# Two-layer Perceiver kernel: in the second attention GpSimd makes every low half, and the FFN weight rounding moves to the expert stage

## The reference, cut to what matters

```
x = x + _L0_xattn_ref(_layernorm(x), ctx_1024, mask, ...)      # attention 1, 6272 keys, masked
x = x + _L0_attn_ref(_layernorm(x), ...)                       # self-attention of the 64 tokens
x = x + _L0_ffn_ref(_layernorm(x), ...)                        # 8 experts, top 2 of a router
x = x + _L1_xattn_ref(_layernorm(x), ctx_1024, ...)            # attention 2: 6272 keys, no mask; then one over x
x = x + _L1_attn_ref(_layernorm(x), ...)                       # delta rule, FIR filters, gate
x = x + _L1_ffn_ref(_layernorm(x), W_in, b_in, W_out, b_out)   # weights rounded to 8 bits, activations to 16

def quantize_w8_per(w, axis):
    amax = jnp.clip(jnp.max(jnp.abs(w), axis=axis, keepdims=True), 1e-08, None)
    scale = 127.0 / amax
    w_q = jnp.clip(jnp.round(w * scale), -128.0, 127.0) / scale
```

## Time and profile before

| | |
|---|---|
| time, median of 3 runs | 408.29 us (408.04 to 408.51) |
| the profiled execution: its time, its span | 407.28 us, 405.5 us |
| busy: PE, DVE, ACT, POOL | 383.2, 286.6, 287.9, 237.8 us |
| attention 2, 222 to 342 us: busy PE, DVE, ACT, POOL | 116.84, 92.46, 106.12, 95.55 us |
| experts, 189 to 208 us: busy PE, DVE, ACT, POOL | 17.80, 11.09, 8.55, 1.65 us |

### The profile page before, as it was taken

One profiled execution on the slowest core, in us unless ns is written; L12 is line 12 of the kernel. 1 busy time (PEld: TensorE's weight loads), 2 busy tenths in 40 slices (PEclk: granted clock), 3 DMA queues, 4 the chain that ended last, 5 costly groups with the idle time before them and its releaser, 6 DMA issues.

```text
span 405.5 us, 11389 instructions
## 1 busy us (share of the span) xinstructions
PE 383.2 (95%) x4529; PEld 280.3 (69%) x4529; DVE 286.6 (71%) x724; ACT 287.9 (71%) x568; POOL 237.8 (59%) x198
## 2 busy tenths in 40 slices
PE   6988999999998999989999999999999999999996
PEld 3435777777776778954955767777777778867843
DVE  3788888888876777556767767877887776455544
ACT  3377888888787887736439989899889987534240
POOL 2497989999974659301006987887787659030000
PEclk9899999999999999999999999999999999999999
DMA  8899998989999997990004999999999999700000
GB/s 310 324 254 167 200 178 138 167 155 212 235 176 214 201 208 132 341 411 21 3 2 92 197 191 195 191 193 190 185 194 214 184 207 182 286 2 2 4 1 5
DMA packets 188390, 68.56 MB, mean 169 GB/s; under 512 B 183200, under 2 KB 183984, under 8 KB 187440
## 3 DMA queue, kind: packets, MB, share of 16 engines
q1 hardware_dynamic: 188048, 66.77, 81.5%
q10 hardware_dynamic: 288, 1.05, 0.7%
HBM read 21.90 MB, written 0.03 MB: 54 GB/s over the span
## 4 chain that ended last, share of the span: by engine, by line
PE 54%; DVE 16%; DMA 10%; POOL 6%; issue 6%; ACT 6%; SPq 2%; POOLq 0%; DVEq 0%; ACTq 0%
PE ps L522 19%; PE ps L490 15%; DMA probsT<-halves 8%; DVE probs L641 7%; POOL halves L594 4%; PE ps L502 3%; ACT probs L559 2%; PE ps L1104 2%; PE ps L766 2%; DMA moe<-in_ctxT 2%; ACT halves L566 1%; SPq L421 1%; PE ps L1212 1%; DVE halves L594 1%; PE ps L826 1%
## 5 line engine op out<-in xcount | busy, mean ns | idle before, releaser
L594 POOL TENSOR_TENSOR halves<-probs,halves 128x896 f16<-128x896 f32 x75 | 141.6, 1892 | 55.1 <-ACT halves L566 53.7
L522 PE MATMUL ps<-ctxN,probsT 128*128 128x128 f16 x2352 | 148.6, 219 | 4.5 <-DMA probsT<-halves 4.1
L522 PEld LDWEIGHTS ps<-ctxN,probsT 128*128 128x128 f16 x2352 | 139.4, 98 | 18.3 <-issue 7.8
L490 PE MATMUL ps<-ctxT_parts,GT_parts 128*128 128x512 f16 (+1 forms) x660 | 143.0, 353 | 5.4 <-DVE negmax L641 5.2
L559 ACT ACTIVATE probs<-probs,shifted 128x896 f32<-128x896 f32 x112 | 115.5, 1031 | 6.7 <-DVE shifted L646 6.7
L490 PEld LDWEIGHTS ps<-ctxT_parts,GT_parts 128*128 128x128 f16 x660 | 59.6, 98 | 57.0 <-DVE negmax L641 8.1
L566 ACT CAST halves<-probs 128x896 f16<-128x896 f32 x93 | 85.8, 923 | 0.0
L654 DVE SCALAR_TENSOR_TENSOR U<-U,alpha,ps 128x128 f32<-128x128 f32 x112 | 38.6, 345 | 54.5 <-PE ps L522 54.2
L641 DVE CUSTOM_DVE_ANT_0 probs<-ps,zero,negmax 128x896 f32<-128x896 f32 x56 | 67.5, 1205 | 1.6 <-POOL halves L594 1.2
L641 DVE CUSTOM_DVE_ANT_0 probs<-ps,maskb,negmax 128x896 f32<-128x896 f32 x56 | 67.5, 1205 | 1.6 <-issue 0.7
L556 ACT ACTIVATE alpha<-negmax 128x1 f32<-128x1 f32 x96 | 28.2, 294 | 37.0 <-DVE negmax L641 35.9
(11 more groups left out here) (369 smaller groups left out, 380.0 us busy)
## 6 DMA issues: line engine op xcount, KB each, us to landing
moe<-in_ctxT SPq DMA_DIRECT2D x7, 448.0 KB, 7.2
moe<-in_mask SPq DMA_DIRECT2D x6, 448.0 KB, 10.1
moe<-in_gateT SPq DMA_DIRECT2D x2, 1024.0 KB, 9.2
moe<-in_upT SPq DMA_DIRECT2D x2, 1024.0 KB, 10.9
moe<-in_downT SPq DMA_DIRECT2D x2, 1024.0 KB, 12.8
moe<-in_fir_long SPq DMA_DIRECT2D x1, 2048.0 KB, 10.3
probsT<-halves SPq DMA_TRANSPOSE x93, 4.7
wv<-in_wv SPq DMA_DIRECT2D x2, 512.0 KB, 6.8
```

Of the source, the lines that this page charges most:

```text
L490: ins = pe.matmul(ps[:, 2 * b + h, 0:width], GT_parts[:, g_part, r * P:(r + 1) * P], ctxT_parts[:, keys:keys + width], start=(g_part == 0 ...
L522: ins = pe.matmul(ps[:, bank, 0:D], probsT_parts[:, b, p_part, k * P:(k + 1) * P], ctxN_parts[:, at:at + D], start=(p_part == 0 and c_part ...
L594: eng.tensor_tensor(halves_of(L, n)[:, 1, :], probs[:, n % BUFS, :], halves_of(L, n)[:, 0, :], ALU.subtract).then_inc(lower_of(L, n)[0], 1)
```

## The change

Three edits. In attention 2, `on_vector` is False for every step, so the nine low halves that VectorE made (steps 15, 19, ... 47) are GpSimd's. The eight operations of `quantise_weights` leave the attention loop and stand in GpSimd's list behind norm 2's power and ahead of `bound_pool(pool, 1)`. And `wqi` and `wqo` are views of `maskb`, so the first operation waits for the last step of attention 1.

```diff
-RAMP = 12
@@
-        wqi = late(P, FT, D)
-        wqo = late(P, FT, D)
+        wqi, wqo = (maskb[:, 2 * k * FT * D:2 * (k + 1) * FT * D].bitcast(F32).rearrange("p (f d) -> p f d", f=FT)
+                    for k in range(2))
@@ def on_vector(L, n):
             if L == 0:
                 return n in (0, 2) or 4 <= n < 30 and n % 4 == 1
-            return n >= RAMP and n % 4 == 3
+            return False
@@ @block.gpsimd
                 if i == 3:
+                    pool.wait_ge(sem("negmax_ready"), STEPS)
+                    for stage in range(8):
+                        quantise_weights(stage // 4, stage % 4)
                     bound_pool(pool, 1)
                 norm_pool(pool, i)
@@
-                        if 12 <= n < 44 and n % 4 == 0:
-                            quantise_weights((n - 12) // 16, (n - 12) // 4 % 4)
```

## The result

The changed kernel takes 410.06 us (median of 7 runs, 408.83 to 412.06) against 408.29 of the kernel before (7 runs): ratio 1.0046, 95% interval 1.0029 to 1.0064, so slower by about 1.9 us. That is 0.26 us above the top of the predicted range. The profiled execution has 409.14 us, span 407.3; before it was 407.28 and 405.5. Its 1.8 us are what is to be explained.

The account below looks back on a forecast made before the run. TensorE was taken to bound the kernel, with attention 2's stalls due to DMA. The median 408.29 - 0.3 (attention 2) + 0.87 (L747 stopped) gave 408.85 us; the 8-in-10 range was 406.3 to 409.8.

Parts of the forecast that it names:

- What bounds the kernel, and attention 2's stalls: Whole kernel and attention 2: TensorE, busy 383.2 of 405.5 us, bounds it; the stalls are DMA's, low halves mostly without effect.
- an even supply: Attention 2, steps 15 to 43: low halves coming evenly from GpSimd could win 2.15 us at most.
- rival 2: Attention 2: stalls come from uneven low halves, so the change wins 2.15 us, 407.0 or 406.1 us in all; chance 0.20.
- -0.3 in attention 2: Steps 30 to 39: about half of 0.54 us won, where SyncE idled because a low half came late.
- L747 stopped, +0.87: Norm 2's xn on VectorE, held by GpSimd's first two-tensor weight operation, ends at 192.18 instead of 191.31: +0.87 us.
- Rival 1: Norm 2: L747 isn't stopped, as GpSimd starts later or no shared port is needed; 408.0 us, chance 0.20.
- The other VectorE operations ... Nothing for them: Router and its weights: VectorE's other two-input operations fall beside scalar GpSimd operations or have room, so they cost 0.
- Rival 3: Router: GpSimd's scalar operations also hold up VectorE's small ones; about +5.8 us, 413.8 us in all, chance 0.10.
- its sign: Router's end: TensorE's L1124 starting after 199 us in the later profile would show the router was stopped.

Follow-up runs that it names:

- e5: e4 with the nine low halves of attention 2 back on VectorE; 408.23 us, ratio 1.0016 to the kernel before.
- e4: Changed kernel, first four weight operations waiting for the router's choice, last four behind norm 3; 407.22 us, ratio 0.9991 to the kernel before.
- e8: e4 with nine one-column memsets in VectorE's list where its low halves had stood; 408.01 us, ratio 1.0006 to the kernel before.
- The probe: Kernel before, with single GpSimd operations (scalar, multiply, copy) beside chains of small VectorE operations added behind its result; no whole-kernel time given.
- e7: Changed kernel with each scalar weight operation replaced by two two-tensor multiplies, no rounding or clip; 412.94 us, ratio 1.0134 to the kernel before.
- e3: Changed kernel with the eight weight operations also waiting until VectorE's xn of norm 2 is done; 407.27 us, ratio 0.9989 to the kernel before.

## Why the prediction was wrong

**What bounds the kernel, and attention 2's stalls: right.** In the 103 us from step 0 to 43 an even supply won nothing: 103.04 before, 103.20 after, 102.79 to 103.84 in the other versions. The stalls stayed DMA's (2.5 us before and after), and rival 2 is out. The trace of the kernel before says more of them than the prediction did: its instruction queue q8 has a packet of some 16 KB every 10 to 12 us (at 246.9, 256.5, 268.25, 280.4, 292.1, 302.2, 313.6 and 323.3), and of the eight pv starts between steps 10 and 43 that come over 2.4 us behind the one before, seven (249.00, 258.59, 270.43, 282.54, 294.31, 315.64, 325.42) lie 2.0 to 2.2 us behind such a packet. The break of the earlier trace rows belongs to the third. That these fetches cause the stalls was not tested.

**-0.3 in attention 2: wrong in size and cause.** The stretch that I gave it to (steps 30 to 39) gained nothing. The last twelve steps gained 1.03 (medians: 1.0 between e5 and e4), by what the profiles show because VectorE's list became nine instructions shorter and a fetch of 8 KB fell between tiles. e8 takes it back with memsets. Without this gain, whose cause the prediction didn't have, the miss would have been some 1.3 us and not 0.26: that it is so small is luck.

**L747 stopped, +0.87: the mechanism right, the size 0.70.** `xn` took 1.05 us and ended 0.08 us behind GpSimd's multiply, where I had 0.21 from the larger low half. Rival 1 is out.

**"The other VectorE operations ... Nothing for them": this step failed.** It put the router's part at nothing, and the router cost 1.39 beyond its slack. It rested on "two-tensor operations of GpSimd stop such an operation of VectorE, scalar ones don't", and that on one row, the low half at 48.36, which lies wholly within 46.61 to 49.83. The probe shows that the middle is the one part of a scalar operation in which VectorE goes on. A row that I hadn't used says as much, the low half at a scalar operation's start. Timelines of the kernel before, VectorE and then GpSimd:

```profile
25.82 1.27 DVE L594 TENSOR_TENSOR halves<-probs,halves 128x896 f16<-128x896 f32 x1
```

```profile
25.22 3.22 POOL L1385 TENSOR_SCALAR maskb<-moe 128x896 bf16<-128x896 int32 x1
```

1.27 in place of 1.08, begun 0.6 us behind the start: stopped for 0.19, until some 0.8 us behind it. (In attention 2 itself the mean of 1.26 hid the same: VectorE's low halves at 258.87 and 297.26, each begun beside a low half of GpSimd, took 1.75 and 1.77, those that met none took 1.08.) Beside that I placed the router wrongly: it met the two multiplies as well, since once `xn` is late the router moves onto them. Measured 1.39 beyond the slack, 0.05 at the start of L1123, and 0.35 behind it. Predicted 0.57 in all; measured -1.03 + 0.16 + 2.49 + 0.25 of drift = 1.87.

**Rival 3** had the right place and threshold ("as soon as the router is over 1.3 us late": 1.29 is what was covered), and its sign came, TensorE's sum after 199 us (199.13). Its price was too large: with passages in the middle of scalar operations the router is 3.4 us late (2.7 by its own stops, 0.7 by `xn`), not 7. e7, in which every operation has two tensors, comes to its 5.8 (22.46 - 16.45 = 6.0), in part by the clock.

The rule of the Trainium skill ("SBUF — State Buffer", section "Who interferes with whom"), that the first holds the shared ports for its whole instruction, agrees with the multiply and the copy (1.20 and 0.53 us, to their ends). For the scalar operation the measurement decides: held at both ends, free in the middle.

The change does no harm when its parts are placed well: e2 (low halves alone, 407.19 us) is faster than before by 0.07 to 0.3%, the only version below before whose interval stays clear of 1. e3, with one wait more than the changed kernel, is at 407.27, and its interval just reaches 1; e4's (407.22) does too, so the three can't be told apart. What e2 gains lies in the last twelve steps (0.8 us), where the fetch fell elsewhere; it doesn't show that an even supply of low halves helps.

## What to carry to other kernels

An idle engine is not free room: GpSimd's operation can stop the VectorE operations that it meets (here tensor_scalar, a cast, and tensor_tensor with both inputs in SBUF), and what has to be read is which ones it meets, how long it holds, and whether their slack is longer than the sum of stops. One row in which two operations ran side by side says nothing about their starts and ends; look for a row of each before calling work hidden. And a gain of 1 us after taking instructions out may be that of a code fetch that fell elsewhere: put empty instructions in their place before believing in a cause.

## What the runs showed of the hardware

- GpSimd's scalar operation of 128x512 (1.94 us) stops such VectorE operations in about its first 0.4 us and, for most, its last 0.3 to 0.4; a multiply of two tensors (1.04 to 1.26) and a copy (0.61) for their whole length.
- VectorE's FIND_INDEX8 (0.16) at the start of GpSimd's scalar operation, and MAX8 (0.17), FIND_INDEX8 (0.16), a reciprocal (0.16) and an operation with one input in PSUM (0.74) beside its multiply, took their usual times.
- One 8 KB packet of instructions is followed by 0.65 us in which the transposes move 5 to 10 GB/s in place of 280. The break at 268.7, 1.3 us long, stands behind a larger one, some 16 KB by the trace (268.2).
- A wait of TensorE of 3.34 us was followed by 3.7 us at a granted clock of 0.58, one of 1.37 us by a clock of 1.00 (one case each).
